# A mixture-of-experts stage that loads an expert's weights only where a buffer holds another expert's

## The chip, the cores and the metric

One NeuronCore of a Trainium2 chip runs one program. Its engines are TensorE (PE), VectorE (DVE), ScalarE (ACT), GpSimd (POOL) and SyncE (SP, which here only issues transfers); sixteen DMA engines move data between HBM and SBUF. The metric is the device time of one execution in microseconds. Lower is better.

## The reference, cut to what matters

Input x is 8 x 512 rows of 256. Both halves start from the layer-normed rows xn: an attention with 16 heads and relative positions, and a mixture of experts whose output gates it.

```python
# attention: B = 8, S = 512, H = 16 heads of D = 16
scores = q k^T
rel_q  = einsum('bhld,lrd->bhlr', q, pos_emb)     # pos_emb = dist_emb[l - r + 255]
rel_k  = einsum('bhrd,lrd->bhlr', k, pos_emb)
probs  = softmax((scores + rel_q + rel_k) / 4)
# experts: NE = 8, F = 1024, the two best of each of the 4096 rows
probs  = softmax(flat @ router_w);  topw, topi = top_k(probs, 2)
h   = silu(einsum('td,edf->tef', flat, w1) + b1)  # w1: 8 x 256 x 1024, b1: 8 x 1024
y   = einsum('tef,efd->ted', h, w2) + b2          # w2: 8 x 1024 x 256, b2: 8 x 256
out = einsum('te,ted->td', combine, y)
result = x + attention(xn) * silu(experts(xn))
```

## The kernel before, in words

Four stages follow one another, each a block that all engines leave before the next one begins: `project` (norms, Q and K), `route` (V, the router, the sorting of rows by expert), `experts`, and `attention`.

`route` writes every row twice, once for each chosen expert, into `sorted`, ordered by expert. Its DVE part `finish` divides each expert's rows into blocks of TB = 256 and fills two tables over NBLK = 40 slots: `owner`, the expert of a slot's block, and `row_of`, the block's first row. The slots of one expert stand next to one another. The reference's router, evaluated on the inputs, gives the eight experts 1219, 782, 1644, 1259, 390, 436, 717 and 1745 rows, so 5, 4, 7, 5, 2, 2, 3 and 7 blocks: slots 0 to 34. Slots 35 to 39 hold no rows, and `owner` is capped at 7 for them; they are computed like the others.

`experts` runs the 40 slots in order. For a slot, PE turns 256 rows (`turn_rows`, L1037), multiplies by w1 (L1049, 1 MB), ACT applies bias b1 and silu (L961), PE multiplies by w2 (L1062, 1 MB), and DVE adds bias b2 into `yo` (L997). Weights, biases and rows have two buffers each, by the slot's parity. POOL issues all their transfers, on its own queue. During slot jb it waits until ACT has read w1's last product and issues the rows, b1 and w1 of slot jb + 2 (`load_first`); when `yo` of slot jb is written it issues b2 and w2 of slot jb + 2 (`load_second`) and then stores `yo` (L942). `owner_of` and `row_at` read a table entry into a register first. It loads both weights for every slot, whoever owned the buffer.

Between the matmuls of the experts, the same stage computes the relative scores of the attention. They are 16 tiles; a tile has 16 units with `krows` (here called its K phase: PE L1028 with tabk, ACT copies into `rel_tile`, L953) and then 16 units with `qrows` (its add phase: PE L1028 with tabq, DVE adds, L976, and SP stores 512 KB, L904). `due` spreads the 512 units evenly over the slots, 12.8 for each, so a tile lasts 2.5 slots and each phase 1.25. The order on PE is fixed in the program: a unit that is not ready holds up the expert matmuls behind it.

SP issues the relative part's transfers in one order: K rows (`load_k`, L884: six transfers of 64 KB for two units, into a ring of KRING = 3 buffers), then the 16 stores of the tile (L904, SRING = 6 buffers in SBUF), every fourth tile with 48 loads of Q rows between them (L889). A K-row buffer is asked for again when PE has done its two units. The K rows of a tile's first six units are asked for in the K phase of the tile before; the others stand behind that tile's stores.

Of the kernel before, what the change touches and what calls it, by code (L numbers as in the profile page):

```python
# [14 lines left out]
I32 = mybir.dt.int32  # L15
# [375 lines left out]
def route(nc, t, keep):  # L391

    with ExitStack() as ctx:
# [5 lines left out]

        ident, cols = keep["ident"], keep["cols"]  # L400
        xn, xnT, wvm, rms2 = keep["xn"], keep["xnT"], keep["wvm"], keep["rms2"]
        y_slots, pair_w, owner, row_of = keep["slots"], keep["pair_w"], keep["owner"], keep["row_of"]
        slots = sb("row_slots", [P, TOPK, NT], I32)
        shift_f, y_slot_f = sb("shift_f", [P, NE]), sb("y_slot_f", [P, TOPK, NT])
        vm = [ctx.enter_context(nc.psum_tensor(f"v_mix{i}", [P, 2 * E], F32)) for i in range(4)]
# [24 lines left out]
        void_f, void = sb("void_f", [P, NE]), sb("void", [P, NE], I32)  # L430
        passed = sb("passed", [P, NBLK, NE])
        owner_f, begun, row_f = sb("owner_f", [P, NBLK]), sb("begun", [P, NBLK]), sb("row_f", [P, NBLK])
        blank = sb("blank", [P, E])
        by_head = [sb(f"by_head{i}", [KS, H, 2 * TILE], BF16) for i in range(2)]
        by_row = sb("by_row", [KS, 2 * TILE, BH], BF16)
# [162 lines left out]
        def _(dve):  # L598
# [87 lines left out]
            def finish():  # L686
                dve.wait_ge(s_cnt, B // 2 + 1)
                then(nc.vector.tensor_scalar(whole_i[:], cnt[:, 1], float(TB - 1), None, ALU.add))
                then(nc.vector.tensor_tensor(void_f[:], cnt[:, 1], first_row[:], ALU.add))
                then(nc.vector.tensor_scalar(void_f[:], void_f[:], -1.0, None, ALU.add))  # L690
                nc.vector.tensor_copy(void[:], void_f[:]).then_inc(s_void, 1)
                then(nc.vector.tensor_scalar(whole_i[:], whole_i[:], TB_SHIFT, None, ALU.logical_shift_right))
                then(nc.vector.tensor_copy(blocks[:], whole_i[:]))
                then(nc.vector.tensor_tensor_scan(ends[:], ones[:, 0:NE], blocks[:], 0.0, ALU.mult, ALU.add))
                then(nc.vector.tensor_tensor(passed[:], ends[:].unsqueeze(1).to_broadcast([P, NBLK, NE]),
                                             turn_no[:].unsqueeze(2).to_broadcast([P, NBLK, NE]), ALU.is_le))
                then(nc.vector.tensor_reduce(owner_f[:], passed[:], AX.X, ALU.add))
                then(nc.vector.tensor_tensor(passed[:], passed[:], ends[:].unsqueeze(1).to_broadcast([P, NBLK, NE]), ALU.mult))
                then(nc.vector.tensor_reduce(begun[:], passed[:], AX.X, ALU.max))
                then(nc.vector.tensor_tensor(begun[:], turn_no[:], begun[:], ALU.subtract))  # L700
                then(nc.vector.tensor_scalar(begun[:], begun[:], float(TB), None, ALU.mult))
                then(nc.vector.scalar_tensor_tensor(row_f[:], owner_f[:], float(CAP), begun[:], ALU.mult, ALU.add))
                v.did(nc.vector.tensor_copy(row_of[:], row_f[:]))
                v.did(nc.vector.tensor_scalar(owner[:], owner_f[:], float(NE - 1), None, ALU.min))
                then(nc.vector.tensor_tensor(shift_f[:], ends[:], blocks[:], ALU.subtract))
                then(nc.vector.scalar_tensor_tensor(shift_f[:], shift_f[:], float(TB), first_row[:], ALU.mult, ALU.subtract))
                then(nc.vector.tensor_scalar(is_first[:], place[:], 0.0, None, ALU.is_gt))
                then(nc.vector.scalar_tensor_tensor(w_first[:], is_first[:], 1.0, shift_f[:].unsqueeze(1).to_broadcast([P, NT, NE]),
                                                    ALU.mult, ALU.mult))
                then(nc.vector.tensor_tensor(place[:], place[:], w_first[:], ALU.add))  # L710
                then(nc.vector.tensor_tensor(place[:], place[:], is_first[:], ALU.add))
                then(nc.vector.tensor_reduce(first_of[:], place[:], AX.X, ALU.max))
                then(nc.vector.tensor_reduce(all_of[:], place[:], AX.X, ALU.add))
                v.did(nc.vector.tensor_scalar(y_slot_f[:, 0], first_of[:], -1.0, None, ALU.add))
                then(nc.vector.tensor_tensor(y_slot_f[:, 1], all_of[:], first_of[:], ALU.subtract))
                then(nc.vector.tensor_scalar(y_slot_f[:, 1], y_slot_f[:, 1], -1.0, None, ALU.add))
                v.did(nc.vector.tensor_copy(y_slots[:], y_slot_f[:]))
                then(nc.vector.tensor_tensor(is_first[:], place[:], first_of[:].unsqueeze(2).to_broadcast([P, NT, NE]), ALU.is_equal))
                then(nc.vector.tensor_tensor(w_first[:], comb[:], is_first[:], ALU.mult))
                then(nc.vector.tensor_reduce(pair_w[:, 0], w_first[:], AX.X, ALU.add))  # L720
                then(nc.vector.tensor_tensor(w_first[:], comb[:], w_first[:], ALU.subtract))
                then(nc.vector.tensor_reduce(pair_w[:, 1], w_first[:], AX.X, ALU.add))
# [101 lines left out]
def experts(nc, t, keep):  # L824

    with ExitStack() as ctx:
# [4 lines left out]
            return ctx.enter_context(nc.semaphore(name))  # L831

        ident, owner, tabq, tabk = keep["ident"], keep["owner"], keep["tabq"], keep["tabk"]
        row_of, cols = keep["row_of"], keep["cols"]
        up = [ctx.enter_context(nc.psum_tensor(f"up{i}", [P, 2, TB], F32)) for i in range(2)]
        dn = ctx.enter_context(nc.psum_tensor("dn", [P, 2, E], F32))
        tp = ctx.enter_context(nc.psum_tensor("tp", [P, KC, TB], F32))
        rl = [ctx.enter_context(nc.psum_tensor(f"rl{i}", [P, 2, 512], F32)) for i in range(2)]

        w1 = [sb(f"w1_{i}", [P, KC, F]) for i in range(2)]  # L840
        w2 = [sb(f"w2_{i}", [P, FC, E]) for i in range(2)]
        b1 = [sb(f"b1_{i}", [P, FC]) for i in range(2)]
        b2 = [sb(f"b2_{i}", [P, E]) for i in range(2)]
        xr = [sb(f"rows{i}", [P, 2, E]) for i in range(2)]
        xT = sb("rowsT", [P, KC, TB])
        hid = sb("hid", [P, FC, TB])
# [64 lines left out]
        def _(pool):  # L911
            def load_first(jb, slot, e1):
                row = row_at(jb)
                pool.dma_start(xr[slot][:], t["sorted"][bass.ds(row, TB)].rearrange("(t p) e -> p t e", p=P)).then_inc(s_x[slot], 16)
                pool.dma_start(b1[slot][:], t["b1"][bass.ds(e1, 1)].rearrange("o p f -> p (o f)")).then_inc(s_x[slot], 16)
                pool.dma_start(w1[slot][:], t["w1"][bass.ds(e1, 1)].rearrange("o (k p) f -> p (o k) f", p=P)).then_inc(s_w1[slot], 16)

            def load_second(slot, e1):
                pool.dma_start(b2[slot][:], t["b2"][bass.ds(e1, 1)].partition_broadcast(P).rearrange("p o e -> p (o e)")).then_inc(s_w2[slot], 16)  # L919
                pool.dma_start(w2[slot][:], t["w2"][bass.ds(e1, 1)].rearrange("o (k p) f -> p (o k) f", p=P)).then_inc(s_w2[slot], 16)  # L920

            def owner_of(jb):
                return pool.value_load(owner[0:1, bass.ds(jb, 1)], min_val=0, max_val=NE - 1)
# [4 lines left out]
            for jb in range(2):  # L928
                e1 = owner_of(jb)
                load_first(jb, jb, e1)  # L930
                load_second(jb, e1)

            for jb in range(NBLK):
                slot = jb % 2
                if jb + 2 < NBLK:
                    e1 = owner_of(jb + 2)
                    pool.wait_ge(s_h, (jb + 1) * FC)
                    load_first(jb + 2, slot, e1)
                    pool.wait_ge(s_y, jb + 1)
                    load_second(slot, e1)  # L940
                pool.wait_ge(s_y, jb + 1)
                pool.dma_start(t["ysorted"][bass.ds(jb * TB, TB)].rearrange("(t p) e -> p t e", p=P), yo[slot][:]).then_inc(s_ys[slot], 16)  # L942
            for i in range(2):
# [3 lines left out]
        def _(act):  # L947
# [7 lines left out]

            for jb in range(NBLK):
                slot = jb % 2
                act.wait_ge(s_x[slot], (jb // 2 + 1) * 32)
                for f in range(FC):
                    act.wait_ge(s_up, jb * (FC // 2) + f // 2 + 1)  # L960
                    nc.scalar.activation(hid[:, f], up[f // 2 % 2][:, f % 2], ACT.Silu, bias=b1[slot][:, f:f + 1]).then_inc(s_h, 1)  # L961
# [6 lines left out]
        def _(dve):  # L968
# [17 lines left out]
            for jb in range(NBLK):  # L986
# [6 lines left out]
                    relative(jb, spot)  # L993
                dve.wait_ge(s_dn, jb + 1)
                after(dve, s_ys[slot], jb // 2 * 16)
                dve.wait_ge(s_w2[slot], (jb // 2 + 1) * 32)
                nc.vector.tensor_tensor(yo[slot][:], dn[:], b2[slot][:].unsqueeze(1).to_broadcast([P, 2, E]), ALU.add).then_inc(s_y, 1)  # L997

        @block.tensor
        def _(pe):  # L1000
# [29 lines left out]

            def turn_rows(jb):
                slot = jb % 2
                pe.wait_ge(s_x[slot], (jb // 2 + 1) * 32)
                after(pe, s_xt, jb * KC)
                for k in range(KC):
                    for i in range(2):
                        last = nc.tensor.transpose(tp[:, k, i * P:(i + 1) * P], xr[slot][:, i, k * P:(k + 1) * P], ident[:])  # L1037
                last.then_inc(s_tp, 1)

            turn_rows(0)  # L1040
            for jb in range(NBLK):
# [11 lines left out]
                        relative(jb, f // 2)  # L1053
                if jb + 1 < NBLK:
                    turn_rows(jb + 1)
                pe.wait_ge(s_w2[slot], (use + 1) * 32)
                after(pe, s_y, jb)
                for i in range(2):
                    for f in range(FC):
# [383 lines left out]
def program(nc, t):  # L1443
    with ExitStack() as ctx:
        def sb(name, shape, dt=F32):
# [7 lines left out]
            "slots": sb("slots", [P, TOPK, NT], I32),  # L1453
            "pair_w": sb("pair_w", [P, TOPK, NT]),
            "owner": sb("owner", [P, NBLK], I32),
            "bo": sb("bo_all", [P, E]),
            "row_of": sb("row_of", [P, NBLK], I32),
        }
# [62 lines left out]
```

## Time and profile before

| | |
|---|---|
| runs | 2170.81, 2171.78, 2174.97 us; median 2171.78 |
| span of the profiled execution | 2176.3 us |
| `project` and `route` | to about 418 us |
| `experts`, first weight matmul to last `yo` | 430.1 to 1433.3 us |
| `attention` | from about 1434 us to the end |
| PE, DVE, ACT, POOL busy | 77%, 52%, 48%, 29% of the span |
| moved by DMA | 576.93 MB |

The page gives one execution; its span is the only time that the profile has of it, 0.2% above the median of the runs. Start times are in us from the span's start. A row of the windows gives, for a stretch, each engine's busy us and number of instructions, the mean granted TensorE clock (1.00 is 2.4 GHz, 0.50 is 1.2 GHz), the mean busy share of the 16 DMA engines and GB/s.

### The profile page before, as it was taken

What the parts mean: (1) busy time and instruction counts of PE and PEld (TensorE: products, weight loads), DVE (VectorE), ACT (ScalarE), POOL (GpSimd) and SP (SyncE); (2) the same over time, 40 slices, a digit from 0 to 9 for tenths busy, and PEclk for the clock granted to TensorE, in tenths of its full rate; (3) what the DMA queues carried; (4) which work ended last, traced back from release to release, by engine and by line L of the source; (5) the groups of instructions that cost most, each with busy time, mean ns of one, the idle gap of its engine ahead of it and who ended that gap; (6) DMA issues with size and microseconds to landing.
All of it is one profiled execution on the core that took longest, in us unless ns stands there. A gap on an engine that the chain in (4) does not pass through costs nothing. (4 is left out here: it accounts for less than half of the span.)

```text
span 2176.3 us, 32607 instructions
## 1 busy us (share of the span) xinstructions
PE 1668.5 (77%) x11256; PEld 1215.5 (56%) x11256; DVE 1132.0 (52%) x3004; ACT 1032.8 (47%) x2029; POOL 624.4 (29%) x708
## 2 busy tenths in 40 slices
PE   6757420178988989869898998858888989889881
PEld 3324210067777777757787777735555555555550
DVE  6655525013344433324444333358887888888870
ACT  3424204034432334424342443437887887887860
POOL 1343351211111111111111111125024535535535
PEclk9878555598999999989998999979999999999995
DMA  5564475699999889889999899789879889889831
GB/s 197 174 231 151 130 217 135 196 256 299 317 314 342 289 301 297 291 298 333 323 326 310 293 314 305 255 311 354 261 252 319 293 265 309 293 278 325 295 116 39
DMA packets 247732, 576.93 MB, mean 265 GB/s; under 512 B 40016, under 2 KB 86608, under 8 KB 246160
## 3 DMA queue, kind: packets, MB, share of 16 engines
q1 hardware_dynamic: 201856, 414.22, 57.3%
q0 software_dynamic: 44560, 152.23, 22.1%
q10 hardware_dynamic: 1152, 8.39, 1.0%
q8 instruction: 90, 1.47, 0.3%
q14 instruction: 74, 0.61, 0.1%
HBM read 371.27 MB, written 203.42 MB: 264 GB/s over the span
## 5 line engine op out<-in xcount | busy, mean ns | idle before, releaser
L976 DVE TENSOR_TENSOR rel_out<-rl,rel_tile 128x1024 f32<-128x1024 f32 x256 | 308.0, 1222 | 250.0 <-PE rl L1028 173.1
L1244 ACT ACTIVATE scores<-scores,row_least 128x512 f32<-128x512 f32 x512 | 365.7, 717 | 23.8 <-DVE row_least L1278 20.5
L1278 DVE CUSTOM_DVE_ANT_1 scores<-sc,rq 128x512 f32<-128x512 f32 x512 | 336.6, 687 | 29.9 <-issue 28.0
L1380 PE MATMUL pt<-ident,scores 128*128 128x128 f32 x2048 | 323.0, 281 | 36.2 <-ACT probsT L1249 17.3
L953 ACT COPY rel_tile<-rl 128x1024 f32<-128x1024 f32 x256 | 249.6, 1017 | 210.6 <-PE rl L1028 172.0
L1049 PE MATMUL up<-rowsT,w 128*128 128x256 f32 x1280 | 330.0, 403 | 4.1 <-DMA w<-in_w 4.1
L1062 PE MATMUL dn<-w,hid 128*128 128x256 f32 x1280 | 328.4, 402 | 0.0
L961 ACT ACTIVATE hid<-up,b 128x256 f32<-128x256 f32 x320 | 134.1, 470 | 399.2 <-PE up L1049 398.6
L1380 PEld LDWEIGHTS pt<-ident,scores 128*128 128x128 f32 x2048 | 250.5, 145 | 112.8 <-DVE probsT L1284 50.5
L1049 PEld LDWEIGHTS up<-rowsT,w 128*128 128x128 f32 x1280 | 243.2, 200 | 33.5 <-issue 4.5
L1062 PEld LDWEIGHTS dn<-w,hid 128*128 128x128 f32 x1280 | 243.6, 201 | 29.2
L1372 PE MATMUL sc<-ks,qs 96*128 96x512 bf16 x512 | 206.7, 404 | 30.3 <-DMA ks<-scratch_parts 19.0
L1028 PE MATMUL rl<-tabk,krows_sb 96*128 96x128 bf16 x2048 | 155.7, 229 | 91.9 <-DMA krows_sb<-scratch_stack 85.3
L1028 PEld LDWEIGHTS rl<-tabk,krows_sb 96*128 96x128 bf16 x2048 | 136.7, 103 | 127.8 <-DMA krows_sb<-scratch_stack 94.9
L1249 ACT COPY probsT<-pt 128x512 f32<-128x512 f32 x256 | 147.3, 575 | 120.0 <-PE pt L1380 112.7
L1284 DVE COPY probsT<-pt 128x512 f32<-128x512 f32 x256 | 175.7, 686 | 7.5 <-PE pt L1380 7.1
L1028 PE MATMUL rl<-tabq,qrows_sb 96*128 96x128 bf16 x2048 | 147.3, 222 | 29.9 <-DVE rel_out L976 29.7
L982 DVE TENSOR_SCALAR rowsT<-tp,cols_sb 128x256 f32<-128x256 f32 x80 | 39.6, 537 | 248.1 <-PE tp L1037 248.1
L1028 PEld LDWEIGHTS rl<-tabq,qrows_sb 96*128 96x128 bf16 x2048 | 130.5, 99 | 58.3 <-DVE rel_out L976 30.1
L1393 PE MATMUL cx<-probsT,vs 128*32 128x512 f32 x1024 | 141.0, 625 | 27.4 <-issue 25.6
L919 POOL DMA_DIRECT2D b<-in_b x40 | 22.8, 569 | 464.1 <-DVE yo L997 464.1
L1372 PEld LDWEIGHTS sc<-ks,qs 96*128 96x128 bf16 x512 | 57.9, 113 | 157.4 <-issue 91.9
(184 smaller groups left out, 1732.8 us busy)
## 6 DMA issues: line engine op xcount, KB each, us to landing
scratch_rel<-rel_out SPq DMA_DIRECT2D x256, 512.0 KB, 8.7
rq<-scratch_rel SPq DMA_DIRECT2D x256, 512.0 KB, 5.2
w<-in_w POOLq DMA_DIRECT2D x80, 1024.0 KB, 10.8
krows_sb<-scratch_stack SPq DMA_DIRECT2D x768, 64.0 KB, 5.4
scratch_parts<-part SPq DMA_DIRECT2D x96, 128.0 KB
by_head<-scratch_parts SPq DMA_DIRECT2D x16, 768.0 KB, 5.7
scratch_stack<-by_row SPq DMA_DIRECT2D x4, 3072.0 KB
qrows_sb<-scratch_stack SPq DMA_DIRECT2D x192, 64.0 KB, 8.2
```

The costliest lines, as they stand in the source:

```text
L953: nc.scalar.copy(both[:, :, u * UN:(u + 1) * UN], rl[r][:].rearrange("p a (b l) -> p l (a b)", l=TILE)).then_inc(s_kc, 1)
L976: nc.vector.tensor_tensor(out[n % SRING][:], rl[r][:].rearrange("p a (b s) -> p (a b) s", s=TILE), both[:, u * UN:(u + 1) * UN], ALU.add). ...
L1028: last = nc.tensor.matmul(dst, lhs, rhs, start=True, stop=True)
L1049: mm = nc.tensor.matmul(up[f // 2 % 2][:, f % 2], w1[slot][:, c, f * P:(f + 1) * P], xT[:, c], start=(c == 0), stop=(c == KC - 1))
L1062: mm = nc.tensor.matmul(dn[:, i], hid[:, f, i * P:(i + 1) * P], w2[slot][:, f], start=(f == 0), stop=(f == FC - 1))
L1244: nc.scalar.activation(sm[j][:, i], sm[j][:, i], ACT.Exp, bias=least[:, j, i:i + 1], scale=-1.0, accum_out=es[:, g // 2 % 2, i, 2 * j + g ...
L1249: nc.scalar.copy(turned(n // HG, n % HG, r), pt[r % 2][:]).then_inc(s_pa, 1)
L1278: nc.vector.tensor_tensor_reduce(sm[j][:, i].rearrange("p (c s) -> p c s", c=LT), sc[i % 2][:].rearrange("p (c s) -> p c s", c=LT), rq[j][ ...
L1284: nc.vector.tensor_copy(turned(n // HG, n % HG, r), pt[r % 2][:]).then_inc(s_pd, 1)
L1372: nc.tensor.matmul(sc[i % 2][:], qs[g % 2][:, j].rearrange("k (p t) -> k t p", t=ST)[:, i], ks[g % 2][:, j], start=True, stop=True).then_i ...
L1380: last = nc.tensor.transpose(pt[r % 2][:, i * P:(i + 1) * P], sm[n % HG][:, i, r * P:(r + 1) * P], ident[:])
L1393: last = nc.tensor.matmul(cx[o % 2][32 * k:32 * (k + 1)], v, turned(g, k, r), start=(r == 0 and g % 2 == 0), stop=(r == ST - 1 and g % 2 = ...
```

## The change

`finish` fills a third table, `fresh`: 1 for slots 0 and 1, and for the others 1 where slot jb's owner (after the cap) is not that of slot jb - 2, the slot that used the same buffers.
In HBM, w1 and b1 of an expert stand as 128 rows of 8224 B, and w2 and b2 (b2 repeated for every row) as 128 rows of 9216 B, so that one transfer brings each pair. The separate bias transfers are gone, and with them their share of the semaphores; ACT's wait for b1 is now a wait for w1's transfer.

```diff
@@ route, finish()
-                v.did(nc.vector.tensor_scalar(owner[:], owner_f[:], float(NE - 1), None, ALU.min))
+                v.did(nc.vector.memset(fresh_f[:, 0:2], 1.0))
+                then(nc.vector.tensor_scalar(owner_f[:], owner_f[:], float(NE - 1), None, ALU.min))
+                v.did(nc.vector.tensor_copy(owner[:], owner_f[:]))
+                then(nc.vector.tensor_tensor(fresh_f[:, 2:NBLK], owner_f[:, 2:NBLK], owner_f[:, 0:NBLK - 2], ALU.not_equal))
+                v.did(nc.vector.tensor_copy(fresh[:], fresh_f[:]))
@@ experts
-        w1 = [sb(f"w1_{i}", [P, KC, F]) for i in range(2)]
-        w2 = [sb(f"w2_{i}", [P, FC, E]) for i in range(2)]
-        b1 = [sb(f"b1_{i}", [P, FC]) for i in range(2)]
-        b2 = [sb(f"b2_{i}", [P, E]) for i in range(2)]
+        first = [sb(f"w1_b1_{i}", [P, KC * F + FC]) for i in range(2)]
+        second = [sb(f"w2_b2_{i}", [P, FC * E + E]) for i in range(2)]
+        w1 = [w[:, 0:KC * F].rearrange("p (k f) -> p k f", k=KC) for w in first]
...
             def load_first(jb, slot, e1):
                 row = row_at(jb)
                 pool.dma_start(xr[slot][:], t["sorted"][bass.ds(row, TB)].rearrange("(t p) e -> p t e", p=P)).then_inc(s_x[slot], 16)
-                pool.dma_start(b1[slot][:], t["b1"][bass.ds(e1, 1)].rearrange("o p f -> p (o f)")).then_inc(s_x[slot], 16)
-                pool.dma_start(w1[slot][:], t["w1"][bass.ds(e1, 1)].rearrange("o (k p) f -> p (o k) f", p=P)).then_inc(s_w1[slot], 16)
-
-            def load_second(slot, e1):
-                pool.dma_start(b2[slot][:], t["b2"][bass.ds(e1, 1)].partition_broadcast(P).rearrange("p o e -> p (o e)")).then_inc(s_w2[slot], 16)
-                pool.dma_start(w2[slot][:], t["w2"][bass.ds(e1, 1)].rearrange("o (k p) f -> p (o k) f", p=P)).then_inc(s_w2[slot], 16)
+                pool.dma_start(first[slot][:], t["w1"][bass.ds(e1, 1)].rearrange("o p f -> p (o f)"), cond=is_fresh(jb)).then_inc(s_w1[slot], 16)
+
+            def load_second(jb, slot, e1):
+                pool.dma_start(second[slot][:], t["w2"][bass.ds(e1, 1)].rearrange("o p f -> p (o f)"), cond=is_fresh(jb)).then_inc(s_w2[slot], 16)
+
+            def is_fresh(jb):
+                if jb < 2:
+                    return None
+                return pool.value_load(fresh[0:1, bass.ds(jb, 1)], min_val=0, max_val=1)
...
-                act.wait_ge(s_x[slot], (jb // 2 + 1) * 32)
+                act.wait_ge(s_w1[slot], (jb // 2 + 1) * 16)
...
-                pe.wait_ge(s_x[slot], (jb // 2 + 1) * 32)
+                pe.wait_ge(s_x[slot], (jb // 2 + 1) * 16)
...
-                pe.wait_ge(s_w2[slot], (use + 1) * 32)
+                pe.wait_ge(s_w2[slot], (use + 1) * 16)
```

Only POOL and DVE get other instructions. On POOL, in the middle of the experts stage, one slot's issues stand like this before (a TENSOR_LOAD with its ISA rows reads a table entry into a register; w_0 and b_0 are w1, b1, and below them b2, w2, of the even slots):

```order
L926 TENSOR_LOAD row_of
L926 ISA x2
L914 ISA
L914 DMA rows<-scratch_sorted 128x2x256
L915 ISA
L915 DMA b_0<-in_b 128x8
L916 ISA
L916 DMA w_0<-in_w 128x2x1024
L919 ISA
L919 DMA b_0<-in_b 128x256
L920 DMA w_0<-in_w 128x8x256
L942 DMA scratch_ysorted<-yo 128x2x256
```

and like this in the changed kernel:

```order
L936 TENSOR_LOAD row_of
L936 ISA x2
L921 ISA
L921 DMA rows<-scratch_sorted 128x2x256
L930 TENSOR_LOAD fresh
L930 ISA x2
L922 ISA
L922 DMA w_b_0<-in_w 128x2056
L930 TENSOR_LOAD fresh
L930 ISA x2
L925 ISA
L925 DMA w_b_0<-in_w 128x2304
```

Two bias transfers have left and two table reads have come, each directly ahead of a weight transfer; the rows and the stores of `yo` keep their places.

On DVE, in `finish`, the rows that write the tables stand like this in the changed kernel (before, one TENSOR_SCALAR at L704 stood in place of the five from the MEMSET to the second CAST):

```order
L704 CAST row_of<-row_f 128x40
L705 MEMSET fresh_f 128x2
L706 TENSOR_SCALAR owner_f<-owner_f 128x40
L707 CAST owner<-owner_f 128x40
L708 TENSOR_TENSOR fresh_f<-owner_f 128x38
L709 CAST fresh<-fresh_f 128x40
L710 TENSOR_TENSOR shift_f<-ends,blocks 128x8
```

Four more small instructions stand ahead of the rest of `finish`.

## Rows read from the trace of the kernel before

**Rows 1.** The page: busy us by engine, and DMA busy tenths in 40 slices.

```profile
PE 1668.5 (77%) x11256; PEld 1215.5 (56%) x11256; DVE 1132.0 (52%) x3004; ACT 1032.8 (47%) x2029; POOL 624.4 (29%) x708
DMA  5564475699999889889999899789879889889831
```

**Rows 2.** Windows of the experts stage, cut at the ends of slots.

```profile
430.10:514.67 84.57, 71.28 (x508) 60.51 (x509) 23.90 (x25) 30.43 (x46) 10.24 (x15) 0.87 1.00 295
514.67:568.33 53.66, 48.81 (x372) 42.03 (x370) 22.32 (x23) 19.25 (x31) 8.24 (x12) 0.94 0.90 298
568.33:612.61 44.28, 40.71 (x326) 35.13 (x325) 13.84 (x15) 20.28 (x30) 8.25 (x12) 0.96 0.93 287
612.61:663.86 51.25, 45.72 (x353) 39.23 (x351) 15.28 (x17) 22.64 (x34) 8.25 (x12) 0.93 0.90 299
663.86:795.17 131.31, 112.04 (x853) 96.56 (x852) 46.14 (x48) 46.95 (x73) 20.61 (x30) 0.90 0.90 304
795.17:843.34 48.17, 41.40 (x321) 35.62 (x320) 18.82 (x19) 16.59 (x27) 8.25 (x12) 0.93 0.96 319
843.34:915.99 72.65, 66.16 (x533) 56.98 (x533) 27.40 (x29) 30.48 (x47) 12.37 (x18) 0.98 0.91 301
915.99:1070.56 154.57, 131.36 (x1029) 112.76 (x1028) 63.46 (x64) 51.00 (x82) 24.77 (x36) 0.93 0.92 316
1070.56:1093.57 23.01, 18.85 (x146) 16.24 (x145) 1.69 (x3) 12.65 (x18) 4.14 (x6) 0.93 0.92 277
1093.57:1134.50 40.93, 40.74 (x343) 35.85 (x343) 22.23 (x22) 15.26 (x26) 8.24 (x12) 1.00 0.98 349
1134.50:1433.31 298.81, 261.73 (x2047) 225.27 (x2044) 113.56 (x114) 111.67 (x172) 44.14 (x64) 0.95 0.89 300
```

**Rows 3.** The window of slots 11 and 12 alone.

```profile
723.65:764.23 40.58, 40.58 (x343) 35.83 (x343) 22.23 (x22) 15.27 (x26) 8.25 (x12) 1.00 0.98 346
```

**Rows 4.** Waits in 430 to 1430: us in total, times, longest us.

```profile
PE rl L1028 <- DMA krows_sb<-scratch_stack: 85.3, 25, 11.1
DVE rel_out L976 <- DMA scratch_rel<-rel_out: 76.1, 52, 6.6
```

**Rows 5.** Slot 10: the timeline's row after a stall, and windows around it.

```profile
712.59 1.89 PE L1028 MATMUL rl<-tabk,krows_sb 96*128 96x128 bf16 x16 [8.12 <-DMA krows_sb<-scratch_stack]
...
694.00:704.00 10.00, 10.00 (x84) 8.88 (x83) 0.99 (x2) 8.70 (x14) 2.68 (x4) 1.00 1.03 392
704.00:712.00 8.00, 0.47 (x3) 0.06 (x1) 0.00 (x0) 0.08 (x1) 1.44 (x3) 0.73 1.05 282
712.00:718.00 6.00, 5.41 (x27) 4.51 (x28) 0.00 (x0) 1.93 (x2) 0.00 (x0) 0.51 0.64 197
```

**Rows 6.** DMA in 430 to 1430; issues: KB each, median us to landing.

```profile
DMA packets 97551, 303.99 MB, mean 304 GB/s; under 512 B 23587, under 2 KB 23587, under 8 KB 97467
...
q0 software_dynamic: 30820, 108.44, 35.7%
...
scratch_rel<-rel_out SPq DMA_DIRECT2D x253, 512.0 KB, 8.7
w<-in_w POOLq DMA_DIRECT2D x76, 1024.0 KB, 10.8
krows_sb<-scratch_stack SPq DMA_DIRECT2D x750, 64.0 KB, 5.4
...
rows<-scratch_sorted POOLq DMA_DIRECT2D x38, 256.0 KB, 5.9
```

**Rows 7.** The K-row loads by line, 430 to 1430: ns min/median/max, then landing.

```profile
L884 SPq DMA_DIRECT2D krows_sb<-scratch_stack x750: 302/420/2114, 437.0 to 1399.5; - x188
...
DMA to landing us min/median/max: 2.0/5.4/14.1
```

**Rows 8.** A table read on POOL, ns min/median/max.

```profile
L926 POOLq TENSOR_LOAD <-row_of x40: 286/372/1005, 418.9 to 1370.0; - x40
```

**Rows 9.** Timeline: DVE's first instruction in the experts stage.

```profile
426.06 0.99 DVE L982 TENSOR_SCALAR rowsT<-tp,cols_sb 128x256 f32<-128x256 f32 x2 [40.82 <-PE tp L1037]
```

More of the change, by code:

```diff
@@ L401, in route @@
         xn, xnT, wvm, rms2 = keep["xn"], keep["xnT"], keep["wvm"], keep["rms2"]
-        y_slots, pair_w, owner, row_of = keep["slots"], keep["pair_w"], keep["owner"], keep["row_of"]
+        y_slots, pair_w, owner, row_of, fresh = keep["slots"], keep["pair_w"], keep["owner"], keep["row_of"], keep["fresh"]
         slots = sb("row_slots", [P, TOPK, NT], I32)
@@ L432, in route @@
         owner_f, begun, row_f = sb("owner_f", [P, NBLK]), sb("begun", [P, NBLK]), sb("row_f", [P, NBLK])
+        fresh_f = sb("fresh_f", [P, NBLK])
         blank = sb("blank", [P, E])
@@ L833, in experts @@
         ident, owner, tabq, tabk = keep["ident"], keep["owner"], keep["tabq"], keep["tabk"]
-        row_of, cols = keep["row_of"], keep["cols"]
+        row_of, cols, fresh = keep["row_of"], keep["cols"], keep["fresh"]
         up = [ctx.enter_context(nc.psum_tensor(f"up{i}", [P, 2, TB], F32)) for i in range(2)]
@@ L838, in experts @@
         rl = [ctx.enter_context(nc.psum_tensor(f"rl{i}", [P, 2, 512], F32)) for i in range(2)]
-        w1 = [sb(f"w1_{i}", [P, KC, F]) for i in range(2)]
-        w2 = [sb(f"w2_{i}", [P, FC, E]) for i in range(2)]
-        b1 = [sb(f"b1_{i}", [P, FC]) for i in range(2)]
-        b2 = [sb(f"b2_{i}", [P, E]) for i in range(2)]
+        first = [sb(f"w1_b1_{i}", [P, KC * F + FC]) for i in range(2)]
+        second = [sb(f"w2_b2_{i}", [P, FC * E + E]) for i in range(2)]
+        w1 = [w[:, 0:KC * F].rearrange("p (k f) -> p k f", k=KC) for w in first]
+        b1 = [w[:, KC * F:KC * F + FC] for w in first]
+        w2 = [w[:, 0:FC * E].rearrange("p (k e) -> p k e", k=FC) for w in second]
+        b2 = [w[:, FC * E:FC * E + E] for w in second]
         xr = [sb(f"rows{i}", [P, 2, E]) for i in range(2)]
@@ L930, in _ @@
                 load_first(jb, jb, e1)
-                load_second(jb, e1)
+                load_second(jb, jb, e1)
             for jb in range(NBLK):
@@ L939, in _ @@
                     pool.wait_ge(s_y, jb + 1)
-                    load_second(slot, e1)
+                    load_second(jb + 2, slot, e1)
                 pool.wait_ge(s_y, jb + 1)
@@ L995, in _ @@
                 after(dve, s_ys[slot], jb // 2 * 16)
-                dve.wait_ge(s_w2[slot], (jb // 2 + 1) * 32)
-                nc.vector.tensor_tensor(yo[slot][:], dn[:], b2[slot][:].unsqueeze(1).to_broadcast([P, 2, E]), ALU.add).then_inc(s_y, 1)
+                dve.wait_ge(s_w2[slot], (jb // 2 + 1) * 16)
+                nc.vector.tensor_tensor(yo[slot][:], dn[:], b2[slot].unsqueeze(1).to_broadcast([P, 2, E]), ALU.add).then_inc(s_y, 1)
         @block.tensor
@@ L1455, in program @@
             "owner": sb("owner", [P, NBLK], I32),
+            "fresh": sb("fresh", [P, NBLK], I32),
             "bo": sb("bo_all", [P, E]),
@@ L1493 @@
         "wo": wo.reshape(2, P, E).transpose(1, 0, 2),
-        "w1": a["L0_ffn_w1"], "w2": a["L0_ffn_w2"],
-        "b1": a["L0_ffn_b1"].reshape(NE, FC, P).transpose(0, 2, 1),
+        "w1": np.concatenate([a["L0_ffn_w1"].reshape(NE, KC, P, F).transpose(0, 2, 1, 3).reshape(NE, P, KC * F),
+                              a["L0_ffn_b1"].reshape(NE, FC, P).transpose(0, 2, 1)], axis=2),
+        "w2": np.concatenate([a["L0_ffn_w2"].reshape(NE, FC, P, E).transpose(0, 2, 1, 3).reshape(NE, P, FC * E),
+                              np.repeat(a["L0_ffn_b2"][:, None], P, axis=1)], axis=2),
         "tri": np.triu(np.ones((P, P), np.float32), 1), "turn_no": np.arange(NBLK, dtype=np.float32),
-        "b2": a["L0_ffn_b2"],
         "bqk": np.stack([a["L0_attn_bq"], a["L0_attn_bk"]]).reshape(2 * KC, P).T,
```

## The prediction

> **What bounds the kernel now.** I read the page first. PE is busy for 77% of the span, the highest of the engines, and the DMA strip stands mostly at 8 or 9 tenths from the ninth slice on [rows 1]: two candidates, and a share of busy time can't choose between them. The change touches the experts stage, so I cut that stage by windows at the ends of slots [rows 2]. The reader is to see three columns there: in 1003.2 us (430.10 to 1433.31) PE is busy for 878.8, its clock lies between 0.87 and 1.00, and the DMA share is 0.89 to 1.00 everywhere.
>
> The floor comes from two neighbouring slots in which nothing goes wrong: slots 11 and 12 take 40.58 us, PE busy for all 40.58 and at clock 1.00 [rows 3]. That is 20.29 us for a slot, and 40 x 20.29 = 811.6 us for the stage. The stage loses 1003.2 - 811.6 = 191.6 us, to an idle PE and to a slow clock.
>
> What PE waits for is in the waits [rows 4]: K rows for 85.3 us; and DVE waits 76.1 us until a store has freed a `rel_out` buffer, which holds up the next units on PE. Both are transfers. One stall shows the chain [rows 5]. From 704 to 712 PE does nearly nothing, while the DMA share is 1.05; it goes on when K rows land, after 8.12 us. The clock falls to 0.5 in the stall and is still 0.51 in the next 6 us, in which PE is busy, so the stall costs about 3 us more than its length. The K rows are small, 64 KB, but they stand behind 512 KB stores on SP's queue and share the DMA engines with POOL's queue, where 1 MB of weights takes 10.8 us to land [rows 6]. So the stage is bound by PE in its best slots and by the DMA engines in the others, and a byte less is worth time only where a stall is.
>
> **What the change takes away.** Every slot from 2 on loads 2 x 1.049 MB of weights and 0.135 MB of biases. The table `fresh` is 1 for 14 of those 38, so 24 loads of 2.23 MB go: 53.6 MB of the 304 [rows 6]. POOL's queue takes 35.7% of 1000 us of all 16 engines for 108.44 MB, or 3.29 us for a MB, so 176 us of DMA time go, out of some 920 that the windows' shares of 0.89 to 1.00 make over 1003 us [rows 2, 6]. What is left, some 744 us, fits under a PE floor of 811.6 us, on average. It need not fit in every phase.
>
> Which stretches lose it: slot jb issues the loads for jb + 2. Slots 3, 4, 7, 8, 14, 15, 19 to 24, 26 and 27 still issue loads; their five windows (514.67, 612.61, 795.17, 915.99 and 1093.57 are their starts) sum to 348.6 us for 14 slots, a loss of 348.6 - 14 x 20.29 = 64.5. The other 26 slots are the six other windows, 654.6 us, a loss of 127.1 [rows 2].
>
> - The first of these, slots 0 to 2, loses 84.57 - 60.87 = 23.7. Both first slots' weights are still loaded at its start, and the clock starts low; three later loads go. I take a third back, 8 us; the bounds are 0 and 23.7.
> - The other 23 slots, 9.2 tiles, lose 103.4 us, or 11.2 a tile. What stays of that I work out by phase. An add phase lasts 1.25 slots, 25.4 us at the floor. It stores 16 x 0.524 = 8.39 MB; the K rows of six units are 1.18 MB; rows and `yo`, 0.524 MB a slot, are 0.66 MB: 10.2 MB. At 392 GB/s, the fullest 10 us that I show [rows 5], that is 26.0 us, at the 346 GB/s of the best slots 29.5 [rows 3]: an excess of 0.6 to 4.1 us a tile. The DMA share in those best slots was 0.98, so I stay near the low end and take 1.3.
> - The K rows of the seventh unit can't be asked for before the buffer is free, four units ahead, 4 x 20.29 / 12.8 = 6.3 us. Six issues at 0.42 and a landing of 2.0 to 5.4 us make 4.5 to 7.9 [rows 7]: a wait of 0 to 1.6; I take 1.0. For the clock after such a wait I take half of what the long stall cost, 1.5.
> - So 1.3 + 1.0 + 1.5 = 3.8 us a tile stay, 35 us in 9.2 tiles; 103.4 - 35 = 68 us come back. The bounds are 103 (nothing stays) and 103.4 - 9.2 x (4.1 + 1.6 + 3.0) = 23.
>
> The 14 slots that still load I leave as they are; fewer transfers from their neighbours help them, and what the new rows of 8 to 9 KB do is a rival below. Bounds: 20 us gained, 32 lost.
>
> The Trainium skill (DMA: Bandwidth & Descriptors, Bandwidth) says that for transfers between HBM and SBUF the HBM side binds, at some 358 GB/s for a core. The trace has 392 over 10 us with reads and writes together [rows 5], so it doesn't agree, and the measurement decides. By the page's figure the 10.2 MB would take 28.5 us, 3.1 us too long a tile in place of my 1.3, and the gain would be smaller by an estimated 17 us.
>
> **What it adds.** POOL reads `fresh` twice a slot, at 0.29 to 1.0 us a read [rows 8], and issues two transfers fewer. POOL is busy for 8.25 us in two slots [rows 3], and its queue has more than a slot's time until the weights are used; 1 to 2 us on it are hidden by POOL's waits. Were that cover gone they would delay `rows`, 40 x 1.5 = 60 us at most. A skipped transfer has no row; I take it at the cost of an issued one or less, from nothing to the price in the slower rival. DVE gets four instructions of about 0.2 us at the end of `route`; DVE then idles 40.82 us before its first instruction in the experts stage [rows 9], so they cost nothing; 0.8 us if that cover were gone. ACT's wait for w1 in place of b1 is one that PE has passed already, since ACT reads what PE made of w1.
>
> **Sum.** 8 + 68 = 76 us. Against the profiled span, 2176.3 - 76 = 2100.3; the median of the runs lies 4.5 lower, so 2171.8 - 76 = 2096. What is late next is PE itself in most slots, and K rows at the start of the K phases that still fall on a weight load.
>
> **The rivals.**
>
> 1. *Nearly everything comes back.* Once backlogs no longer carry from a tile to the next, the add phase drains within its six buffers and the K rows land in 2 us. For it: slots 11 and 12 ran at the floor with the weights still there [rows 3], since the buffers took up the excess. Against it: the phase's need of 10.2 MB in 25.4 us is at the top of what the rows show. Gain 105 to 127: about 2055.
> 2. *Most of the stalls stay,* because stores and K rows fill the DMA engines by themselves, or because the weight rows become larger packets. Now nearly all data packets are of 2 to 8 KB, those of w2's 1 KB rows too [rows 6], so the two queues share the engines packet by packet about evenly. If a row of 8 to 9 KB went as one packet, the K rows would get a third and not a half while a load runs: waits 1.5 times as long, so the 64.5 us of the loading slots become 97, and 76 - 32 = 44 are left. With the low bounds above, 23. The time is about 2137. The Trainium skill (DMA: Bandwidth & Descriptors, Queues, rings and completion order) says that each engine takes turns between queues at the granularity of packets. That speaks against this change if the packets grow; no row here shows it.
> 3. *The condition saves no traffic,* say because the data move and only the count differs. Then all bytes are as before, and the time is that of before, 2172. Only the definition of the operation speaks against it; no row of before has one.
> 4. *Slower: a skipped transfer holds POOL.* The place is POOL's in-order queue, the price that of one skip. POOL has 4.1 us of work a slot [rows 3], and some 1.5 us with the table reads; two skips fit beside it up to (20.3 - 5.6) / 2 = 7.3 us each. Beyond that rows arrive late and POOL sets the slot. The slots without loads take 654.6 / 26 = 25.2 us now, so the point from which it is slower than before is (25.2 - 5.6) / 2 = 9.8 us a skip. At 11, near what a load takes to land (10.8 [rows 6]), a slot takes 27.6, and 24 of them 24 x 2.4 = 58 us more: 2230. An issue of a transfer is far below that in every row, so the chance is small.
>
> **How the numbers follow.** The forecast, a gain of 50 to 105 us, gets 0.62. Rival 1 gets 0.10, rival 2 (10 to 50 us gained) 0.17, rival 3 0.04, rival 4 0.07. The time predicted is 2096. The range runs from 2050 (a gain of 122) to 2142 (a gain of 30): it takes in all of the forecast, most of rival 1 and more than half of rival 2. A difference under 0.2%, 4.3 us, can't be told from none. Faster by more than that is 0.62 + 0.10 + 0.17 = 0.89; the same 0.04; slower 0.07.
>
> **What would show it.** POOL's queue should move about 54 MB less in the stage, and no more, which settles rival 3. The stage, now 1003 us, should be near 927; windows at the slots' ends should show the stretches from 663.86 to 795.17 and from 1134.50 on close to 22 us a slot at a clock of 0.98 or more, and those with loads about as they are. The wait of PE for K rows should fall from 85 to some 35 us, and what remains should stand in K phases that follow slots 4, 7, 14, 19, 22, 24 and 27. POOL's time for a skipped transfer settles rival 4, the count of packets over 8 KB the second half of rival 2. The attention stage should not change. I am wrong if the waits for stores and K rows stay in slots 28 to 39, where no weights move.

## The result, and the profile after

The changed kernel takes 2107.2 us (median of 5 runs, 2103.2 to 2123.2) against 2173.3 (2170.8 to 2176.8): 0.9696 of before, 95% interval 0.9661 to 0.9731. On a second chip the ratio was 0.9723 (0.9681 to 0.9765). It is faster by 66 us; forecast were 76.

The page's DMA strip and the queue of POOL, to be laid beside [rows 1, 6]:

```profile
PE 1641.8 (77%) x11256; PEld 1204.0 (57%) x11256; DVE 1129.5 (53%) x3008; ACT 1032.1 (49%) x2029; POOL 537.5 (25%) x628
...
DMA  6574465688789678788887777589889989999831
```

The strip falls to mostly 7 and 8 tenths in the experts stage and stays about as it was in the attention. In that stage, 426 to 1376:

```profile
DMA packets 77892, 251.96 MB, mean 265 GB/s; under 512 B 21036, under 2 KB 21036, under 8 KB 73881
...
q0 software_dynamic: 10662, 54.73, 18.6%
...
scratch_rel<-rel_out SPq DMA_DIRECT2D x256, 512.0 KB, 4.5
krows_sb<-scratch_stack SPq DMA_DIRECT2D x750, 64.0 KB, 2.4
```

POOL's queue moves 54.7 MB, 53.7 less than the 108.44 of [rows 6]: all that the table said. Stores land in 4.5 us in place of 8.7, K rows in 2.4 in place of 5.4. Some 4000 packets are now of 8 KB and more. (The page's own line on HBM reads shows 371.27 MB for both kernels, and for the one below that loads no weights after slot 1; it goes down to 361.83 MB only where transfers are no longer issued, in the experiment without Q rows. So it counts a skipped load as if it had moved.)

Windows of the stage, cut at the ends of the same slots as in [rows 2] (first slots 0 to 2, 9 to 13, 16 to 18, 19 to 24, 28 to 39, leaving out the others; the last line is the whole):

```profile
426.00:507.55 81.55, 69.88 (x508) 60.04 (x509) 23.82 (x25) 30.58 (x46) 3.82 (x10) 0.88 0.84 252
...
649.96:771.13 121.17, 106.99 (x853) 93.03 (x852) 45.94 (x48) 46.96 (x73) 8.09 (x20) 0.94 0.75 253
...
816.08:879.89 63.81, 63.81 (x533) 56.34 (x533) 27.21 (x29) 30.24 (x47) 5.06 (x12) 1.00 0.75 259
879.89:1041.00 161.11, 131.05 (x1025) 112.64 (x1024) 63.29 (x63) 50.20 (x81) 14.83 (x24) 0.92 0.89 299
...
1108.07:1375.24 267.17, 249.50 (x2048) 218.64 (x2044) 112.84 (x114) 111.59 (x172) 17.20 (x43) 0.97 0.72 248
...
426.00:1375.24 949.24, 857.50 (x6812) 745.75 (x6812) 366.58 (x374) 376.84 (x577) 72.90 (x153) 0.95 0.79 265
```

The stage goes from 1003.2 to 949.2 us. Two long stretches, slots 11 to 13 and 31 to 38, now look like this:

```profile
707.32:771.13 63.81, 63.81 (x533) 56.34 (x533) 27.21 (x29) 30.25 (x47) 4.54 (x12) 1.00 0.70 241
1189.18:1355.12 165.94, 165.94 (x1385) 146.53 (x1385) 72.98 (x76) 77.10 (x119) 11.42 (x30) 1.00 0.68 240
```

PE is busy for every microsecond and its clock is 1.00. The eight slots of the second stretch take 20.74 us each; slots 31 to 35, five slots or one period of the schedule, take 102.1, so 20.4 each. What stays is elsewhere. PE's wait for K rows:

```profile
PE rl L1038 <- DMA krows_sb<-scratch_stack: 66.0, 14, 13.8
```

It is 66.0 us in 14 waits, where it was 85.3 in 25 [rows 4]: fewer waits, and the longest one longer. The longest three, 10.3, 13.8 and 9.8 us, stand in slots 10, 20 and 30; of the others over 1 us, two stand in slots 0 and 1 and the rest in slots 5, 8, 15, 23, 25 and 28. PE's row after the one in slot 10, SP's issues before it, and the DMA engines from 677 to 690:

```profile
696.36 1.89 PE L1038 MATMUL rl<-tabk,krows_sb 96*128 96x128 bf16 x16 [10.30 <-DMA krows_sb<-scratch_stack]
...
680.15 0.89 SPq L911 DMA_DIRECT2D scratch_rel<-rel_out  x2
681.09 4.29 SPq L896 DMA_DIRECT2D qrows_sb<-scratch_stack  x6
685.42 2.16 SPq L911 DMA_DIRECT2D scratch_rel<-rel_out  x2
687.62 3.14 SPq L896 DMA_DIRECT2D qrows_sb<-scratch_stack  x6
690.80 9.22 SPq L891 DMA_DIRECT2D krows_sb<-scratch_stack  x20
...
DMA packets 1298, 4.09 MB, mean 315 GB/s; under 512 B 303, under 2 KB 303, under 8 KB 1297
```

No weights move in slot 10. PE stops at 686.1, and SP asks for the K rows only from 690.8 on, since six Q-row loads stand after every two stores. The stall was there before too, in slot 10 [rows 5], and the forecast put it down to the stores ahead of the K rows and the weights beside them; it did not reckon with the 48 issues of Q rows.

On POOL, the issue of the second weight transfer (the short ones are skipped):

```profile
L925 POOL DMA_DIRECT2D w_b<-in_w x40: 44/44/557, 418.8 to 1332.8; - x40
```

A skipped transfer costs POOL 0.044 us.

Slot 5, from 554.51 to 580.42, shows how a load reaches into the slot behind the one that asks for it. POOL issues w2 for slot 6 when slot 4's `yo` is written; SP asks for the K rows just after, and PE waits for them:

```profile
556.45 0.55 POOL L925 DMA_DIRECT2D w_b<-in_w  x1 [14.17 <-issue]
...
557.37 16.08 SPq L891 DMA_DIRECT2D krows_sb<-scratch_stack  x24
...
568.91 1.89 PE L1038 MATMUL rl<-tabk,krows_sb 96*128 96x128 bf16 x16 [4.03 <-DMA krows_sb<-scratch_stack]
```

### The profile page after: what moved, and what is told of

It reads as the page before. It is cut to its first block and busy times, and to the rows that moved or that the text cites. A ratio compares the mean times of both kernels' runs of the same rounds, so it can differ in the third digit from the quotient of the medians.

```text
span 2121.5 us, 32639 instructions
## 1 busy us (share of the span) xinstructions
PE 1641.8 (77%) x11256; PEld 1204.0 (57%) x11256; DVE 1129.5 (53%) x3008; ACT 1032.1 (49%) x2029; POOL 537.5 (25%) x628
## 3 DMA queue, kind: packets, MB, share of 16 engines
q0 software_dynamic: 24208, 98.65, 14.3%
HBM read 371.27 MB, written 203.42 MB: 271 GB/s over the span
## 5 line engine op out<-in xcount | busy, mean ns | idle before, releaser
L1059 PE MATMUL up<-rowsT,w_b 128*128 128x256 f32 x1280 | 322.1, 396 | 3.3 <-DMA w_b<-in_w 3.3
L1072 PE MATMUL dn<-w_b,hid 128*128 128x256 f32 x1280 | 322.3, 396 | 0.0
L971 ACT ACTIVATE hid<-up,w_b 128x256 f32<-128x256 f32 x320 | 134.3, 471 | 375.5 <-PE up L1059 374.8
L1390 PEld LDWEIGHTS pt<-ident,scores 128*128 128x128 f32 x2048 | 250.4, 145 | 109.0 <-DVE probsT L1294 53.7
L1059 PEld LDWEIGHTS up<-rowsT,w_b 128*128 128x128 f32 x1280 | 237.9, 196 | 31.0 <-issue 3.6
L1072 PEld LDWEIGHTS dn<-w_b,hid 128*128 128x128 f32 x1280 | 239.4, 197 | 27.6
L925 POOL DMA_DIRECT2D w_b<-in_w x40 | 9.9, 248 | 480.5 <-issue 337.0
```

Of the source, the lines that this page charges most:

```text
L1059: mm = nc.tensor.matmul(up[f // 2 % 2][:, f % 2], w1[slot][:, c, f * P:(f + 1) * P], xT[:, c], start=(c == 0), stop=(c == KC - 1))
L1072: mm = nc.tensor.matmul(dn[:, i], hid[:, f, i * P:(i + 1) * P], w2[slot][:, f], start=(f == 0), stop=(f == FC - 1))
L1390: last = nc.tensor.transpose(pt[r % 2][:, i * P:(i + 1) * P], sm[n % HG][:, i, r * P:(r + 1) * P], ident[:])
```

## The experiments

The experiments ran in three groups, each on one chip beside the kernel before: the first four; the changed kernel again with the always-true condition, the Q rows loaded once and the four K-row buffers; and the last four, two of them repeats. The kernel before differs by up to 15 us from chip to chip, so ratios to it are compared across chips, and microseconds only within one.

**Rows alone.** Without a condition, every slot loads.

```diff
-                pool.dma_start(first[slot][:], ..., cond=is_fresh(jb)).then_inc(s_w1[slot], 16)
+                pool.dma_start(first[slot][:], ...).then_inc(s_w1[slot], 16)
```

> The weights and biases in one row per partition, but loaded for every slot, without a condition. Theory (the bytes that don't move are the whole effect): all bytes of before move, so the time is that of before, 2173 us, within 5. Rival (rows of 8 to 9 KB travel as larger packets and crowd out the K rows on the shared DMA engines): K rows wait up to 1.5 times as long in every tile, so 20 to 60 us slower than before, 2193 to 2233.

Measured: 0.9907 (0.9881 to 0.9933). Both theories miss: it is some 20 us faster than before, and not slower. The larger packets do not crowd out the K rows in sum: PE waits 81.3 us for them, 85.3 before. Each slot also sends two transfers fewer than before, the biases' own, so this run does not say that the longer rows are what saves time.

**Condition alone.**

```diff
-        first = [sb(f"w1_b1_{i}", [P, KC * F + FC]) for i in range(2)]
-        second = [sb(f"w2_b2_{i}", [P, FC * E + E]) for i in range(2)]
+        w1 = [sb(f"w1_{i}", [P, KC, F]) for i in range(2)]
+        w2 = [sb(f"w2_{i}", [P, FC, E]) for i in range(2)]
+        b1 = [sb(f"b1_{i}", [P, FC]) for i in range(2)]
+        b2 = [sb(f"b2_{i}", [P, E]) for i in range(2)]
...
+                pool.dma_start(b2[slot][:], ..., cond=new).then_inc(s_w2[slot], 16)
+                pool.dma_start(w2[slot][:], ..., cond=new).then_inc(s_w2[slot], 16)
```

> The condition on all four transfers of a slot (w1, b1, w2, b2), with the separate tensors and rows of before. Theory (the bytes are the whole effect): as the changed kernel, 2107 us, within 5. Rival (larger packets cost time in the 14 slots that load): 8 to 25 us faster than the changed kernel, 2082 to 2099, with packets of at most 4096 B in the trace.

Measured: 0.9699 (0.9659 to 0.9740), against 0.9696 for the whole change. Within the intervals the condition is the whole effect, and the rival, 8 to 25 us faster than the changed kernel, is out.

**No loads after the first two slots.**

```diff
-                then(nc.vector.tensor_tensor(fresh_f[:, 2:NBLK], owner_f[:, 2:NBLK], owner_f[:, 0:NBLK - 2], ALU.not_equal))
+                then(nc.vector.memset(fresh_f[:, 2:NBLK], 0.0))
```

> The changed kernel with the table fresh set to 0 from slot 2 on: no weights are loaded after the first two slots, so the expert outputs are computed with the first experts' weights. Theory: the 14 slots that load fall to the floor of 20.3 us; what stays is the start (about 20 us over the floor) and the three stalls after Q-row loads (slots 10, 20 and 30, about 15 us each with the slow clock), so the stage takes about 877 us in place of 949 and the kernel about 2035. Rival (stores and K rows fill the DMA engines by themselves): at most 20 us faster than the changed kernel, 2087 or more.

Measured: 0.9447 (0.9414 to 0.9480), some 54 us under the changed kernel; the theory said 72, the rival at most 20. The stage:

```profile
428.80:1313.10 884.30, 834.17 (x6812) 732.08 (x6812) 365.80 (x374) 376.33 (x577) 58.22 (x153) 0.97 0.76 249
```

884 us where 877 was expected. The waits for K rows and for free store buffers that are left without any weights:

```profile
PE rl L1038 <- DMA krows_sb<-scratch_stack: 36.0, 5, 10.2
DVE rel_out L986 <- DMA scratch_rel<-rel_out: 20.0, 9, 5.6
```

Three of the five waits for K rows stand in slots 10, 20 and 30, 9.3, 10.2 and 9.2 us long, where they were 10.3, 13.8 and 9.8 in the changed kernel; one of 7.2 us stands in slot 0. In slots 5, 8, 15, 23, 25 and 28 none over 1 us is left. So those of slots 10, 20 and 30 come from weights in a small part at most, and those of the other six do come from them.

**Q rows asked for by ACT.**

```diff
@@ SP
-                    if tile % LT == LT - 1 and tile + 1 < TILES and u % PER_PIECE == PER_PIECE - 1:
-                        load_q(tile // LT + 1, u // PER_PIECE)
@@ ACT, relative()
+                    elif tile % LT == LT - 1 and tile + 1 < TILES and u % PER_PIECE == PER_PIECE - 1:
+                        act.wait_ge(s_qp, tile * UNITS + u + 1)
+                        p = u // PER_PIECE
+                        for i, pair in enumerate(PAIRS):
+                            src = t["stack"][tile // LT + 1, pair[0], :, p * PIECE:(p + 1) * PIECE]
+                            act.dma_start(qst[i * D:(i + 1) * D, p], src).then_inc(s_ql[p], 16)
```

> The changed kernel with the Q rows of every fourth tile asked for by ACT and not by SP, at the same place in the work. Theory (the stalls in slots 10, 20 and 30 are SP's: 48 issues of 0.4 to 0.8 us stand ahead of the K rows on its queue): the stalls of 10.3, 13.8 and 9.8 us go and their slow clock with them, 30 to 45 us faster than the changed kernel, 2062 to 2077. Rival (the DMA engines are full there with 3 MB of Q rows beside the stores): the same bytes at the same time, so within 5 us of 2107.

Measured: 0.9581 (0.9541 to 0.9621), 0.0115 or some 25 us under the changed kernel's 0.9696. More than the rival's 5, less than the theory's 30 to 45. SP's queue in the same tile:

```profile
642.56 29.02 SPq L911 DMA_DIRECT2D scratch_rel<-rel_out  x16
672.80 17.35 SPq L891 DMA_DIRECT2D krows_sb<-scratch_stack  x22
```

The issues of Q rows are off SP. PE's waits for K rows are halved against the changed kernel, and none is over 7.4 us; that one is in slot 0. In their place come waits for ACT, which now issues the Q rows between its other work:

```profile
PE rl L1042 <- DMA krows_sb<-scratch_stack: 32.2, 11, 7.4
...
PE rl L1042 <- ACT rel_tile L961: 11.1, 6, 3.9
...
PE dn L1076 <- ACT hid L975: 10.5, 4, 3.8
```

From slot 9 into slot 10 ACT issues 23 of the Q-row transfers in a row and does nothing else for 15.6 us:

```profile
658.99 15.71 ACTq L968 DMA_DIRECT2D qrows_sb<-scratch_stack  x23
674.80 0.84 ACT L975 ACTIVATE hid<-up,w_b 128x256 f32<-128x256 f32 x2 [15.56 <-issue]
```

The same bytes move, and yet the K-row stalls over 1 us in slots 10 and 30 are gone and that of slot 20 is 2.7 us. So a good part of those stalls was SP's issues and not the bytes, though a wait for ACT can also cover K rows that come late. The slots stay long all the same: slots 9 and 10 take 51.1 us where they took 57.4, since PE stands for ACT there (in the changed kernel it waits 1.1 us in all for `rel_tile` and not at all for `hid`). The 25 us are what is left of the gain after that.

**The changed kernel again,** with a second profile:

> The changed kernel once more, beside the next three on one chip, and with a second profile. By the ratio measured for it, 0.9696 of before. If the first profiled execution (16 us over the median of its runs) was an outlier, this profile's stage takes 925 to 940 us; if the stage is 949 again, the difference lies outside it.

Measured: 0.9723 (0.9681 to 0.9765), 2120.3 us. The stage took 947.9 us again, so the first profile's stage was no outlier. PE's wait for K rows is 64.2 us in 14 times, with the same three slots longest. The profiled execution was the longest of its runs again (2127.1).

**Condition always true.** The memset of the third experiment, with 1.0.

> The changed kernel with the table fresh set to 1 everywhere: every transfer has its condition, and every condition is true. Theory (a true condition costs nothing that the path sees): as the rows alone, 0.991 of before, within 0.003. Rival (the condition itself, or the table read ahead of it, delays the weights or holds POOL): slower than the rows alone by 5 us or more, 0.994 or more.

Measured: 0.9985 (0.9962 to 1.0009), above the rows alone. The two were run again, on one chip:

> The rows alone, without a condition, beside the next two on one chip. On two different chips it stood at 0.991 of before and the version with a condition that is always true at 0.9985. Theory (the gap lay in the chips): this one and the always-true one come out within 0.003 of each other. Rival (the condition costs 15 us by itself): 0.991 here again, and 0.998 there.

Measured: 0.9934 (0.9911 to 0.9958), 2165.3 us.

> The condition always true, rows in one. As said for the rows alone: within 0.003 of them if the condition is free, 0.006 to 0.009 above if it costs 15 us.

Measured: 0.9983 (0.9960 to 1.0006), 2174.0 us. The gap of the first time is there again, at 9 us on one chip: conditions that are true, with the table read ahead of each, cost time, about what the rows save. That is less than the rival's 15 us, and the intervals only just part. The traces put it in the experts stage and give no single place there. PE's wait for K rows and DVE's for free store buffers are, with the rows alone and then with true conditions:

```profile
PE rl L1038 <- DMA krows_sb<-scratch_stack: 83.6, 25, 13.5
DVE rel_out L986 <- DMA scratch_rel<-rel_out: 68.5, 37, 7.0
```

```profile
PE rl L1038 <- DMA krows_sb<-scratch_stack: 88.7, 29, 13.3
DVE rel_out L986 <- DMA scratch_rel<-rel_out: 83.0, 50, 7.1
```

In the first pair the K rows' wait hardly differs (81.3 and 81.9), but that for store buffers rises there too, from 71.5 to 78.0. Why it does is not shown.

> The condition with the tensors and rows of before. If the rows save time on their own, as the first run of the rows alone said (20 us), and the savings add in proportion to the loads that are left (14 of 38), this is 5 to 10 us slower than the changed kernel, 0.974 of before; if the rows bring nothing once the condition is there, 0.970 to 0.972.

Measured: 0.9729 (0.9700 to 0.9759), 2118.1 us, between its two forecasts; the changed kernel's second ratio is 0.9723, so no difference to it can be told. With 14 loads in place of 38, the rows' gain and the condition's cost, if they go by the loads, are an estimated 3 to 7 us each (14 to 20 us and 9 to 17 us, times 14/38), too little to tell here.

**Q rows loaded only for the first tiles.** SP's `load_q` in the stores' loop is left out, with

```diff
-                            pe.wait_ge(s_ql[u // PER_PIECE], (lt + 1) * 16 * len(PAIRS))
+                            pe.wait_ge(s_ql[u // PER_PIECE], 16 * len(PAIRS))
```

> The changed kernel without the Q-row loads of tiles 4, 8 and 12: 144 transfers of 64 KB are left out, and the relative scores of those tiles use the first Q rows. Theory (what slots 9, 10, 19, 20, 29 and 30 lose over 20.4 us comes from the Q rows, by SP's issues and by their bytes): most of their 51 us goes, 35 to 50 us faster than the changed kernel. Of that the version with ACT's issues gave 25, which is the part of the issues; the rest is the bytes. Rival (each K phase after a full add phase stalls in any case): 10 us or less beyond that version.

Measured: 0.9484 (0.9444 to 0.9524), 2066.1 us beside the changed kernel's 2120.3 on the same chip, 54 less. Slots 9 and 10, in the changed kernel and here:

```profile
649.96:707.32 57.36, 43.18 (x321) 36.70 (x320) 18.73 (x19) 16.71 (x27) 3.55 (x8) 0.88 0.80 266
```

```profile
651.84:690.16 38.32, 38.32 (x321) 33.84 (x320) 18.68 (x20) 16.58 (x27) 3.54 (x8) 1.00 0.87 308
```

57.4 us become 38.3, PE busy throughout. The Q rows cost 19 us there, and 54 in the three places together (19 and 20: 19, 29 and 30: 15). By the same windows the version with ACT's issues had brought back 16 of these 54; the other 9 of its 25 us lie elsewhere. A K-row wait of 2.8 us stays in slot 20, as with ACT's issues. How the remaining 38 us divide between the Q rows' bytes and ACT's issues is not shown.

**ACT for the Q rows and four K-row buffers,** then five:

```diff
-KRING = 3
+KRING = 4
```

> ACT asks for the Q rows, and the K rows have four buffers in place of three, so those of a tile's first eight units are asked for ahead of the stores. Theory (what stays in the slots that load is the latency of the seventh unit's K rows behind stores and weights): 3.2 us more of cover for each tile takes away the stalls of 2.5 to 5 us in some seven tiles and shortens the others, 20 to 35 us faster than with ACT's issues alone, 0.942 to 0.949 of before. Rival (the DMA engines are full in those tiles, so a stall is only put off): within 5 us of that version, 0.956 to 0.960.

Measured: 0.9480 (0.9434 to 0.9525), 2067.5 us, 53 under the changed kernel on its chip and 0.010 under the version with ACT alone, some 22 us: the low end of the theory, and far from the rival. PE's wait for K rows falls from 32.2 to 15.0 us.

> ACT asks for the Q rows, and five K-row buffers. Four brought 20 to 25 us over three. Theory (latency of the first K rows behind stores and weights): the fifth covers what four left in slots 5, 8, 15, 23 and 28, 5 to 15 us more, 0.941 to 0.946 of before. Rival (what is left are add phases in which the DMA engines are full): no gain, 0.946 to 0.950.

Measured: 0.9461 (0.9426 to 0.9495), 2060.4 us; no difference to four buffers can be told, and it falls between theory and rival. Its waits show what took over:

```profile
DVE rel_out L990 <- DMA scratch_rel<-rel_out: 36.1, 20, 9.8
...
PE rl L1042 <- DMA krows_sb<-scratch_stack: 6.0, 3, 3.7
```

PE's wait for K rows is down to 6 us, and DVE waits 36 for stores, after 25 with ACT's issues alone and 31 with four buffers. This version beats both kernels, by 5.4% and by some 2.5%.

## Why the prediction was right, point by point

- *Floor.* Right. 20.29 us a slot was forecast; 20.4 is what slots without disturbance take over a period, and two long stretches run there.
- *Bytes.* Right: 53.7 MB measured, 53.6 forecast.
- *Slots 0 to 2.* 8 us were to come back; 84.57 - 81.55 = 3.0 did. The third taken for it came from no row.
- *The 14 loading slots.* Forecast unchanged at 348.6 us; 343.4 by the same windows, and none of rival 2's 32 us were lost.
- *The other 23 slots.* This is the term that was mis-sized: 68 us forecast, 570.1 - 524.3 = 45.8 measured. The working spread one residual, 3.8 us a tile, over all 9.2 tiles. The runs show three kinds. Sixteen of the slots have no residual at all: they take 335.8 us where they took 378.1 (42.3 back), and 335.8 again in the run that loads no weights after slot 1. Slots 9, 10, 29 and 30 gave back 117.9 - 111.0 = 6.9 only, since their stalls are those of the Q rows; without these they take 76.6. Slots 5, 25 and 28 come right behind a slot that loads and gave back nothing (74.1 to 77.5); without weights they take 58.8. w2 of slot jb + 2 is issued only when slot jb's `yo` is written, which is where the windows end slot jb. So about half of a slot's load moves in the slot behind it, as the rows of slot 5 above show. The prediction itself names the K phases behind slots 4, 24 and 27 as places where stalls stay, and its sum counts them among the slots that recover.
- *Latency of the K rows.* 0 to 1.6 us was forecast for every tile, and 1.0 taken. In the sixteen quiet slots it is nothing; it lies in the tiles that meet a load, where a fourth K-row buffer beside ACT's issues brought 22 us.
- *The sum.* In the profiles the stage gives 54.0 us, its start 4.1, and the attention takes 3.3 more: 54.8 of span. The runs' medians give 66. Twice the profiled execution of the changed kernel was the longest of its runs, by 7 and 16 us over their median. Its span lies 14.3 us over the median of the runs, that of before 3.0, and the difference is the 11 us by which the profiles show less than the runs; why it is there is open. In the stage 76 us were forecast and 54 came, but the total misses by 10 only, because of those 11 us, which no trace places. That 66 came so near to 76 is in part luck.
- *Signs.* The stretches named for it came to 24.2 us a slot at a clock of 0.94 and 22.3 at 0.97; 22 at 0.98 was forecast. PE's wait for K rows fell to 66 us and not to 35: it stood in the K phases that the prediction named, behind slots 4, 7, 14, 19, 22, 24 and 27, but also in slots 10 and 30, which it had not named, and those two and slot 20 make 34 of the 66. From slot 31 on no wait for K rows over 1 us is left, so the sign of being wrong did not come.
- *Rivals.* Nearly everything coming back: its mechanism held in the sixteen quiet slots, better than the forecast's residual, and failed in the others; of its 105 us or more, 48.8 came. Stores and K rows filling the engines by themselves: refuted by another 54 us without weights. Packets: they grew, as its condition asked, and the rows alone were faster. The Trainium skill (DMA: Bandwidth & Descriptors, Queues, rings and completion order) has the engines alternate between queues packet by packet. No run here shows the turns themselves; with packets twice as large PE waited 81.3 and 83.6 us for K rows, and 85.3 before, so no loss shows. No saving, and a skip that holds POOL: refuted by 53.7 MB and by 0.044 us.

That the weights made the stalls of the slots now at the floor is shown by the condition alone and by the run without weights. That the Q rows made those of slots 10, 20 and 30 is shown by leaving them out. What in a true condition and its table read costs 9 us is open, as is what in the rows alone saves time, the longer rows or the two transfers fewer.

## What to carry to other kernels

Where one queue's stalls are due to another queue's traffic, a transfer that is skipped gave back the whole stall in the phases that then fit (42 us in sixteen slots here), and little where another load or another cause was left (6 us in the other ten): count by phase, and place each load at the time of its issue, not in the slot that asks for it. Before a stall is put down to bytes in flight, look at when its transfer was asked for; here 48 issues of other rows on the same sequencer came first. Moving them to another engine puts their cost on that engine's work. A buffer more for the small loads that stand behind large stores was worth as much as a third of the change.

## What the runs showed that was not expected

The issue of a w2 transfer costs 0.044 us of POOL with a false condition and 0.547 with a true one, the table read ahead of it not counted. Rows of 8 to 9 KB became packets of 8 KB and more, and the same bytes in such rows, with two transfers a slot fewer, were 0.7 to 0.9% faster than before in two pairs of runs. Conditions that are all true, with their table reads, cost about as much again. With 24 of the 38 loads gone, the longest stall was longer than before, 13.8 us against 11.1, in a slot that still loads.
